# Two taps per VectorE instruction in the sampling stage of a deformable convolution

## The reference

```python
x = x + _L0_conv_ref(_gn(x), ...)          # residual blocks, two deconvolutions
offsets = _conv2d(_gn(x), w_off, b_off)    # 2 offsets (dy, dx) for each of the 9 taps
# for each tap k and pixel: py = y - 1 + ky + dy,  px = x - 1 + kx + dx
# val[k] = bilinear sample of _gn(x) at (py, px), zero outside
x = x + einsum('bckhw,ock->bohw', val, w_def)
```

## Time and profile before

| what | value |
|---|---|
| median of 3 runs | 1282.44 us (1280.95 to 1284.28) |
| span of the profiled execution | 1282.5 us |
| mean granted TensorE clock, share of full speed | 0.954 |
| busy PE, DVE, ACT, POOL | 1055.9, 888.9, 672.1, 62.4 us |
| sampling stage | about 760 to 1270 us |

### The profile page before, as it was taken

The page is one execution under the profiler, slowest core; times in us unless marked ns, Lnnn a source line. Parts: engine busy times, 40 slices in busy tenths (PEclk is TensorE's granted clock), DMA queues, the critical chain, the costliest instruction groups (busy, mean ns, idle before and its releaser), DMA issues.

```text
span 1282.5 us, 41555 instructions
## 1 busy us (share of the span) xinstructions
PE 1055.9 (82%) x16938; PEld 669.3 (52%) x16938; DVE 888.9 (69%) x1378; ACT 672.1 (52%) x907; POOL 62.4 (5%) x89
## 2 busy tenths in 40 slices
PE   0799999987595999999974957888778887888784
PEld 0234446664242455446642426666666766666664
DVE  5877762334988878742528948888878887888870
ACT  0532433112166333331113477888788887988771
POOL 0000000000052000000000440000000000000000
PEclk9999999999797999999998978999999998999997
DMA  8000023150643000211305254443434443444421
GB/s 200 1 1 2 2 96 67 40 128 1 165 106 85 1 1 1 96 34 35 68 1 150 78 135 129 137 135 114 127 111 124 122 132 105 131 130 117 114 81 34
DMA packets 78797, 107.02 MB, mean 83 GB/s; under 512 B 10511, under 2 KB 67047, under 8 KB 75928
## 3 DMA queue, kind: packets, MB, share of 16 engines
q1 hardware_dynamic: 78472, 103.18, 29.9%
q10 hardware_dynamic: 144, 1.18, 0.3%
HBM read 74.85 MB, written 29.47 MB: 81 GB/s over the span
## 4 chain that ended last, share of the span: by engine, by line
issue 45%; PE 38%; DVE 9%; ACT 2%; POOL 2%; DMA 1%; SPq 0%; POOLq 0%; DVEq 0%; ACTq 0%
PE psum L843 23%; PE psum L912 13%; DVE tp L1749 2%; DVE v L1637 2%; DMA x_odd<-x 1%; PE psum L953 1%; DVE stats L1817 1%; POOL offp L2022 1%; POOL offr L2018 1%; ACT xm L1383 1%; PE psum L934 1%; DVE xm L1804 1%; DVE tm L1755 1%; PE psum L943 1%; DVE xm L1688 1%
## 5 line engine op out<-in xcount | busy, mean ns | idle before, releaser
L843 PE MATMUL psum<-v,u 64*64 64x512 f32 x3072 | 337.1, 597 | 19.7 <-DVE v L1637 14.6
L1460 ACT ACTIVATE dist<-psum 128x1024 f32<-128x1024 f32 x288 | 288.8, 1027 | 51.3 <-PE psum L1039 40.1
L843 PEld LDWEIGHTS psum<-v,u 64*64 64x64 f32 x3072 | 148.1, 134 | 207.1 <-issue 190.4
L1850 DVE TENSOR_SCALAR dist<-dist 128x1024 f32<-128x1024 f32 x288 | 202.3, 703 | 73.3 <-ACT dist L1460 71.4
L1086 PE MATMUL psum<-hat,win 64*64 64x144 f32 x4096 | 197.3, 319 | 36.0 <-DVE outt L1886 20.8
L1860 DVE TENSOR_TENSOR hat<-dist 128x512 f32<-128x512 f32 x288 | 195.3, 687 | 0.3
L1160 PE MATMUL psum<-val,wdefs 64*64 64x256 f32 x1944 | 161.2, 392 | 32.1 <-ACT val L1463 23.6
L1086 PEld LDWEIGHTS psum<-hat,win 64*64 64x64 f32 x4096 | 152.3, 136 | 64.2 <-issue 63.3
L1463 ACT ACTIVATE val<-psum 128x864 f32<-128x864 f32 (+3 forms) x230 | 146.8, 677 | 32.6 <-PE psum L1086 24.5
L1039 PE MATMUL psum<-offs,sels 61*64 61x256 bf16 x2304 | 134.7, 283 | 26.2 <-issue 16.3
L1160 PEld LDWEIGHTS psum<-val,wdefs 64*64 64x64 f32 x1944 | 95.4, 137 | 48.4 <-issue 41.2
(11 more groups left out here) (146 smaller groups left out, 988.5 us busy)
## 6 DMA issues: line engine op xcount, KB each, us to landing
win<-pixd SPq DMA_DIRECT2D x256, 68.0 KB
win<-pixd SPq DMA_DIRECT2D x128, 136.0 KB
raw<-x SPq DMA_DIRECT2D x16, 512.0 KB, 7.8
x1d<-xm SPq DMA_DIRECT2D x16, 512.0 KB, 6.0
pixd<-turned SPq DMA_DIRECT2D x64, 128.0 KB, 2.4
x1t<-x1d SPq DMA_DIRECT2D x63, 128.0 KB, 2.7
out<-outt SPq DMA_DIRECT2D x63, 128.0 KB, 2.8
offs<-offd SPq DMA_DIRECT2D x32, 162.0 KB
```

Source lines behind the costliest of these rows:

```text
L843: mm = pe.matmul(o, u4[half, i, v, ky, :], V[half, at:at + CHUNK, cg, v, :], start=start, stop=stop, skip_group_check=True)
L1460: act.activation(dist_at(j, n), psum[:, slot:slot + 2, :], ACT.Abs).then_inc(dist_abs, 1)
L1850: dve.tensor_scalar(d, d, 1.0, 1.0, ALU.min, ALU.subtract).then_inc(hats_made, 1)
```

## The change

The ring becomes three buffers of two taps each. DVE clamps and multiplies the taps 0 and 1, 2 and 3, 4 and 5, 6 and 7 in pairs, with one instruction each, and tap 8 alone: 5 clamps and 5 products a strip in place of 9 and 9. The slots are given by a table for two strips (`PAIR_SLOT`), as ten units don't divide by three. ACT still writes one tap at a time and waits at the first tap of a pair for the product that last used the buffer. Each pair's product follows its own clamp. The result stands between the clamp and the product of taps 4 and 5 (`RESULT_AT = 2` counts pairs), and DVE's copy of group 2 stands after the product of taps 6 and 7 (`DVE_GROUPS_AT = {3: [2]}`). PE and ACT keep their orders, and every group of values stays with the engine that copied it.

```diff
--- before.py
+++ after.py
@@ -78,7 +78,10 @@


 UNITS = TAPS
-DIST_RING = 6
+DIST_RING = 3
+PAIRS_OF = [(0, 2), (2, 4), (4, 6), (6, 8), (8, 9)]
+PAIRS = len(PAIRS_OF)
+PAIR_SLOT = [0, 1, 2, 0, 1, 2, 0, 1, 2, 1]
 TAP_PITCH = BANK + 2
 EDGE_PITCH = W0 + 2
 GROUP_BLOCKS = [(0, 3), (3, 6), (6, 9), (9, 12), (12, 14), (14, 16)]
@@ -88,7 +91,8 @@
 NORMS = 8
 WEIGHED_AT = {1: [0, 1], 2: [2, 3], 3: [4, 5], 4: [6, 7, 8]}
 GROUPS_AT = {5: [0], 6: [1, 2], 7: [3], 8: [4, 5]}
-RESULT_AT = 5
+RESULT_AT = 2
+DVE_GROUPS_AT = {3: [2]}
 VAL_PITCH = W0 + 2
 COLS = 12
 SUM_BANKS = (6, 7)
@@ -276,7 +280,7 @@
         hat_e = in_u4("hat_e", [P, 4 * EDGE_PITCH])
         assert in_u4.at <= WOFF_AT
         in_stage = Map(STAGE_AT)
-        dist = in_stage("dist", [P, DIST_RING, 2, BANK])
+        dist = in_stage("dist", [P, DIST_RING, 2, IMAGES, BANK])
         assert in_stage.at <= V_START
         past_offsets = Map(low.at - size([P, 16, W0], F32))
         hat = past_offsets("hat", [P, 2, (TAPS + K) * TAP_PITCH])
@@ -520,7 +524,12 @@

         def dist_at(j, n):

-            return dist[:, (UNITS * j + n) % DIST_RING]
+            return dist[:, PAIR_SLOT[PAIRS * j + n // 2], n % 2]
+
+        def pair_before(j, i):
+
+            at = PAIRS * j + i
+            return next(back for back in range(1, 2 * PAIRS) if PAIR_SLOT[at - back] == PAIR_SLOT[at])

         block = E(nc.Block())

@@ -1057,7 +1066,7 @@

                 if g == 0:
                     pe.wait_ge(win_in[j], count)
-                    pe.wait_ge(prod_dve, UNITS * (s + 1))
+                    pe.wait_ge(prod_dve, PAIRS * (s + 1))
                     settled(pe)
                 if g >= 2:
                     pe.wait_ge(*group_taken(s, g - 2))
@@ -1449,13 +1458,10 @@
             def absolute(s, j, n, first=False):
                 act.wait_ge(dist_made, UNITS * s + (n + 1))

-                if n >= DIST_RING or not first:
-                    m_ = n - DIST_RING
-                    q = s if m_ >= 0 else s - 1
-                    m_ %= UNITS
-                    act.wait_ge(prod_dve, UNITS * q + (m_ + 1))
-                elif n == DIST_RING - 1:
+                if first and n == 2 * (DIST_RING - 1):
                     act.wait_ge(edge_hats, 1)
+                elif n % 2 == 0 and not (first and n < 2 * DIST_RING):
+                    act.wait_ge(prod_dve, PAIRS * s + (n // 2 + 1 - pair_before(j, n // 2)))
                 slot = 2 * dist_slot(j, n)
                 act.activation(dist_at(j, n), psum[:, slot:slot + 2, :], ACT.Abs).then_inc(dist_abs, 1)

@@ -1508,8 +1514,8 @@
             def edge_absolute(e):
                 act.wait_ge(edge_dist, e + 1)
                 if e:
-                    act.wait_ge(prod_dve, UNITS * STRIPS)
-                act.activation(dist[:, DIST_RING - 1, :, 0:K * W0], psum[:, 0:2, 0:K * W0], ACT.Abs).then_inc(edge_abs, 1)
+                    act.wait_ge(prod_dve, PAIRS * STRIPS)
+                act.activation(dist[:, DIST_RING - 1, 0, :, 0:K * W0], psum[:, 0:2, 0:K * W0], ACT.Abs).then_inc(edge_abs, 1)

             edge_absolute(0)
             for n in range(UNITS):
@@ -1843,24 +1849,29 @@
             dve.wait_ge(far_total, 1)
             dve.tensor_scalar(flag[:], psum[0:1, STAT_BANK, 0:1], 0.0, None, ALU.is_gt).then_inc(flag_set, 1)

-            def hats(s, j, n):
-
-                dve.wait_ge(dist_abs, UNITS * s + (n + 1))
-                d = dist_at(j, n)
+            def hats(s, j, i):
+
+                n0, n1 = PAIRS_OF[i]
+                dve.wait_ge(dist_abs, UNITS * s + n1)
+                d = dist[:, PAIR_SLOT[PAIRS * j + i], 0:n1 - n0]
                 dve.tensor_scalar(d, d, 1.0, 1.0, ALU.min, ALU.subtract).then_inc(hats_made, 1)

-            def product(s, j, n):
-                if n == 0 and not (isinstance(s, int) and s < 2):
+            def product(s, j, i):
+
+                if i == 0 and not (isinstance(s, int) and s < 2):
                     dve.wait_ge(vals_made, GROUPS * (s - 1))
                     settled(dve)
-                dve.wait_ge(hats_made, UNITS * s + (n + 1))
-                d = dist_at(j, n)
-                lo = TAP_PITCH * n + n % K
-                to = hat[:, j, lo:lo + BANK].rearrange("p (b n) -> p b n", b=IMAGES)
-                dve.tensor_tensor(to, d[:, :, 0:PS * HALF_W], d[:, :, PS * HALF_W:], ALU.mult).then_inc(prod_dve, 1)
+                dve.wait_ge(hats_made, PAIRS * s + (i + 1))
+                n0, n1 = PAIRS_OF[i]
+                d = dist[:, PAIR_SLOT[PAIRS * j + i], 0:n1 - n0]
+                first = TAP_PITCH * n0 + n0 % K
+                to = hat[:, j, first:first + BANK]
+                step = TAP_PITCH * (n1 - 1) + (n1 - 1) % K - first
+                to = bass.AP(to.tensor, to.offset, [to.ap[0], [step, n1 - n0], [HALF_STRIP, IMAGES], [1, HALF_STRIP]])
+                dve.tensor_tensor(to, d[:, :, :, 0:HALF_STRIP], d[:, :, :, HALF_STRIP:], ALU.mult).then_inc(prod_dve, 1)

             def edge_product(e):
-                d = dist[:, DIST_RING - 1, :, 0:K * W0]
+                d = dist[:, DIST_RING - 1, 0, :, 0:K * W0]
                 dve.wait_ge(edge_abs, e + 1)
                 if e:
                     dve.wait_ge(edge_made, 1)
@@ -1888,20 +1899,17 @@

             def strip_step(s, j, uses, last=False):

-                for n in range(UNITS):
-                    if n == RESULT_AT and not (isinstance(s, int) and s == 0):
+                for i in range(PAIRS):
+                    if not last:
+                        hats(s + 1, 1 - j, i)
+                    elif i == 0:
+                        edge_product(1)
+                    if i == RESULT_AT and not (isinstance(s, int) and s == 0):
                         strip_result(s - 1, 1 - j, uses if j else uses - 1)
                     if not last:
-                        hats(s + 1, 1 - j, n)
-                        if n > 0:
-                            product(s + 1, 1 - j, n - 1)
-                    elif n == 0:
-                        edge_product(1)
-                    for g in GROUPS_AT.get(n, []):
-                        if g in DVE_GROUPS:
-                            take_group(s, j, g)
-                if not last:
-                    product(s + 1, 1 - j, UNITS - 1)
+                        product(s + 1, 1 - j, i)
+                    for g in DVE_GROUPS_AT.get(i, []):
+                        take_group(s, j, g)

             dve.wait_ge(edge_abs, 1)
             dve.memset(hat_e[:], 0.0).then_inc(edge_step_dve, 1)
@@ -1913,9 +1921,9 @@
                         at_ = lo + K * TAP_PITCH * ky
                         dve.memset(hat[:, j, at_:at_ + K], 0.0)
             edge_product(0)
-            for n in range(UNITS):
-                hats(0, 0, n)
-                product(0, 0, n)
+            for i in range(PAIRS):
+                hats(0, 0, i)
+                product(0, 0, i)

             strip_step(0, 0, 1)
             dve.wait_ge(val_cleared, 1)
```

## The result

The changed kernel takes 1455.6 us (median of 4 runs, 1445.1 to 1460.8), the kernel before 1281.7 us beside it. The ratio is 1.1335, 95% interval 1.1284 to 1.1386. The forecast was 1414, its likeliest case 1385 to 1445 and its whole range 1330 to 1455. So the direction was right and the time was not: it is 41 us above the forecast, outside the likeliest case and 0.6 us past the range's upper end, which is less than the four runs differ among themselves. The profiled execution is the fastest of the four. The mean granted clock is 0.886, before 0.954.

The account below looks back on a forecast made before the run. Bound: a closed loop between ACT, DVE and PE in sampling, no engine full. 1282.5 + 0.6 start and end + 115.5 delays + 20 clock - 4 stalls = 1414.6, taken as 1414 us; range 1330 to 1455.

Parts of the forecast that it names:

- likeliest case: Sampling stage: outt and group 2's copy both come late and TensorE's clock falls; 1385 to 1445 us, 75%.
- The chain and its two late places: DVE-PE-ACT loop in sampling: outt 1.07 us late, group 2's copy behind tap 7; together 3.85 us a step, 115.5 in all.
- Merged instructions at the present rate: DVE: pair clamp 1.22 us, saving 0.56 us a strip, taken back by dependent order; total unchanged within 0.1 us.
- The ring at nothing: ACT's waits for products in the ring of three pairs: covered by over 2 us, costed at nothing.
- TensorE's clock: PE's standstill ahead of group 4 halves the clock: 0.9 us in three steps of four, 20 us; bounds nothing and 60.
- what could go wrong: Low clock reaches into PE's weighing, which has only 0.3 us of cover, and costs more than 0.9 us.
- Stalls of PE's own: PE's stalls in the mean step that fall into the new wait cost nothing any more: -4 us.
- a late copy absorbed: Group 2's late copy is hidden by ACT's and PE's work, only outt's 1.07 us counts: 1315, up to 1350; 10%.
- the slow rate: DVE's long clamp runs at the slow rate, four on the chain, 4.24 us more a step: 1541 us; 5%.
- a gain: DVE's instruction time bounds the loop and each merged pair saves: 1265 us, or 1245 at 1.2 us a strip; 4%.
- no change: Delay and saving on the loop cancel, time the same within 0.3%; 3%.

Follow-up runs that it names:

- longer filling: Changed kernel, PE making tap 6's distances seven times and tap 8's twelve times over, ahead of its two long waits: 1400.2 us, ratio 1.0900.
- both moves: Changed kernel with outt ahead of the clamp of taps 4 and 5 and group 2's copy ahead of the clamp of taps 6 and 7: 1283.5 us, ratio 0.9997.
- copy early: Changed kernel with DVE's copy of group 2 moved ahead of the clamp of taps 6 and 7: 1334.6 us, ratio 1.0391.
- before, copy late: Kernel before, single taps, with DVE's copy of group 2 moved behind the clamp of tap 7 and product of tap 6: 1356.1 us, ratio 1.0563.
- first filling: Changed kernel, PE making tap 6's distances four times and tap 8's seven times over, ahead of its two long waits: 1449.0 us, ratio 1.1292.
- outt early: Changed kernel with outt moved ahead of the clamp of taps 4 and 5, group 2's copy left late: 1414.3 us, ratio 1.1010.

## Why the prediction came out as it did

- *The chain and its two late places* were right, to 0.1 us at each point of the quiet step, and each was shown alone (outt by the copy moved early, the copy by outt moved early and in the kernel before). Without a fall of the clock the forecast gave 1395 us; the kernel with the longer filling, in which the clock hardly falls, takes 1400.2.
- *Merged instructions at the present rate*: 1.22 taken for the clamp, 1.25 measured; product 1.22. DVE's total from start to start was to stay as it was, and it did: a pair takes 825.94 - 823.54 = 2.40 us from its clamp to what follows its product, four single instructions took 4 x 0.60. Its busy time fell by 888.9 - 877.6 = 11.3 us, which made no difference to the time (both moves together: 0.9997). The Trainium skill, page "VectorE: DVE Perf Modes", section "Rules for kernel authors", says to minimise the number of operations. That rule would have given the opposite sign; no run shows a gain from it here.
- *The ring at nothing*: right, from step 1 on no wait of ACT for a product shows.
- *TensorE's clock* is the term that was mis-sized, and with it the sum: 20 us taken (0.9 us in three steps of four), 60 its upper bound, 55 measured. These 35 us are most of the 41 that the forecast is short. Two things in it were wrong. I gave a fall to group 4's standstill alone, while the wait for outt, which I put at 1.6 us and which measured 2.0, brings one of its own (48 falls in some 31 steps; 24 in the run in which it is the only long one). And I priced only groups 4 and 5 at the low level, 0.9 us. In the step with the low clock the cost lies in three places: from outt to tap 7's absolute there are 4.13 us instead of 3.17 (1148.19 to 1152.32, 819.31 to 822.48), from group 4 to the end of ACT's last copies 3.65 instead of 2.74, and from the next A to outt 8.79 instead of 7.90, because the distances of taps 2 and 3 come late out of the weighing. That sums to 2.76, and 18.36 + 2.76 is the 21.1 of that step. The last was named as what could go wrong. The Trainium skill, page "TensorE: Matmul & The Clock Gate", section "HAM oscillation — how this bites in real kernels", tells of a loop whose wait throws the clock back in every pass. On how often it falls that was the better guide, as the trace now shows.
- *Stalls of PE's own*, -4 us: not tested by itself. With the longer filling the mean step is 18.8 - 18.4 = 0.4 to 0.5 us above the quiet one, before the change 0.7, which agrees with a small gain.
- The rivals: a late copy absorbed, the slow rate, a gain, and no change are refuted, by the 94.1 us of waits for the copy, by the 1.25 us of the clamp, and by the time. That the measured time lies near the upper bound of the clock's term, and not at its middle, means that the bound and not the forecast had the clock right.

## What to carry to other kernels

Merging instructions on one engine also moves its hand-written order: look for what was between the merged ones (here a result and a copy on which an in-order PE waits) and place that first. A delay found on a loop between engines must be priced with what the standing engine does afterwards; here the clock added 55 us to 118. A long wait that can't be removed may be cheaper if TensorE is kept busy in it.

## What the runs showed of the hardware

Work for nothing made the kernel faster: 4216 more matmuls, 55 us less. How often TensorE's clock fell goes with how long PE stood still in each step. A standstill is the mean of the waits counted above, and the windows of 1 us begin at 800 us:

| kernel | PE stands for outt, us | for group 2's copy, us | falls of the clock | at the low level, us |
|---|---|---|---|---|
| before | 0.8 | none | 4 in 465 windows | 21 |
| longer filling | 0.8 | 0.8 | 3 in 630 | 27 |
| copy early | 2.0 | none | 24 in 520 | 82 |
| before, copy late | 0.9 | 2.1 | 25 in 540 | 126 |
| first filling | 1.3 | 2.0 | 26 in 630 | 167 |
| changed | 2.0 | 3.1 | 48 in 630 | 222 |
| outt early | 0.5 | 3.3 | 31 in 600 | 242 |

Falls don't all cost the same: 24 in the kernel whose long wait is the one for outt make 82 us at the low level, 31 in the kernel whose long wait is the one for the copy make 242. The two kernels with filling also keep PE busier, so they don't tell the two apart. PE has other, rarer standstills as well; in the kernel before, a fall followed 2.10 us of "issue".

In DVE's work, eight instructions fewer in each strip took 11.3 us off its busy time and, with both moves made, left the kernel's time unchanged; the single ones of 0.69 us had started 0.60 us apart.
